# An added wait ahead of the scatters of a block loop, in a Mamba-2 and mixture-of-experts layer

## What is computed

```python
h = _layernorm(x) * (1 + cb) + sb
scores = sigmoid(h @ gate_w.T)
_, idx = top_k(scores + gate_b, 4)
w = 2.5 * scores[idx] / sum(scores[idx])
for e in range(16):
    y = y + comb[:, e] * ((silu(h @ w13[e, :128].T) * (h @ w13[e, 128:].T)) @ w2[e].T)
y = y + shared expert
x = x + gb * y
```

## Time and profile before

| | |
|---|---|
| median of 3 runs | 1903.9 us (1902.3 to 1906.38) |
| the profiled execution | 1903.56 us, its span 1901.8 us |
| PE busy | 1550.4 us, 82% of the span |
| DVE busy | 1423.9 us, 75% |
| ACT busy | 1092.2 us, 57% |
| POOL busy | 1042.6 us, 55% |
| scatters of the block loop, POOL L2270 | 272, 261.7 us busy, 962 ns each |
| POOL idle before them | 256.3 us |
| DMA engines over the span | 125 GB/s |

### The profile page before, as it was taken

The page is one execution under the profiler, slowest core; times in us unless marked ns, Lnnn a source line. Parts: engine busy times, 40 slices in busy tenths (PEclk is TensorE's granted clock), DMA queues, the critical chain, the costliest instruction groups (busy, mean ns, idle before and its releaser), DMA issues. The chain is left out here.

```text
span 1901.8 us, 35726 instructions
## 1 busy us (share of the span) xinstructions
PE 1550.4 (82%) x10562; PEld 1321.7 (69%) x10562; DVE 1423.9 (75%) x3336; ACT 1092.2 (57%) x2311; POOL 1042.6 (55%) x940
## 2 busy tenths in 40 slices
PE   6749999988888988989898894178888887875798
PEld 4337788777777777777777774067777777775565
DVE  6747899999999999999999995434444444442688
ACT  4635766767767676767676764245555545453222
POOL 2113446566666666666666666725555555554553
PEclk9879999999999999999999996589999999997899
DMA  8620011212121212122121215555555555552998
GB/s 283 211 80 32 25 49 43 79 60 79 62 80 61 80 59 72 64 71 71 61 77 62 75 56 171 187 168 157 168 155 159 154 171 149 162 152 75 373 400 322
DMA packets 149368, 238.24 MB, mean 125 GB/s; under 512 B 27792, under 2 KB 96144, under 8 KB 149008
## 3 DMA queue, kind: packets, MB, share of 16 engines
q1 hardware_dynamic: 123296, 166.20, 27.7%
q0 software_dynamic: 25344, 69.50, 9.9%
q10 hardware_dynamic: 544, 0.26, 0.0%
HBM read 128.66 MB, written 109.35 MB: 125 GB/s over the span
## 5 line engine op out<-in xcount | busy, mean ns | idle before, releaser
L2270 POOL DMA_INDIRECT ys_dram<-byo,bids x272 | 261.7, 962 | 256.3 <-DVE bids L2250 155.1
L1625 DVE SCALAR_TENSOR_TENSOR cv<-xc,convw,cv 128x256 f32<-128x256 f32 x576 | 331.0, 629 | 14.1 <-ACT xc L1476 14.1
L1105 POOL DMA_INDIRECT xs_dram<-rows,dest x256 | 264.5, 1033 | 61.5 <-issue 59.2
L2223 DVE TENSOR_TENSOR bhl<-bank,bhh 128x512 fp32r<-128x512 f32 x136 | 94.1, 692 | 195.9 <-ACT bhh L2175 185.0
L116 PE MATMUL bank<-wh,bhh 128*128 x544 | 161.0, 296 | 77.3 <-ACT bhh L2175 63.6
L2175 ACT ACTIVATE bhh<-bank 128x512 fp32r<-128x512 f32 x136 | 83.5, 614 | 185.2 <-PE bank L2108 177.3
L116 PEld LDWEIGHTS bank<-wh,bhh 128*128 128x128 f32 x544 | 103.0, 189 | 90.7 <-issue 90.7
L117 PE MATMUL bank<-wl,bhh 128*128 x544 | 154.9, 285 | 1.5 <-issue 1.5
L118 PE MATMUL bank<-wh,bhl 128*128 x544 | 154.0, 283 | 0.9 <-issue 0.9
L1945 POOL TENSOR_TENSOR state<-state,par 128x512 f32<-128x512 f32 x64 | 94.7, 1479 | 104.5 <-PE bank L1326 104.4
L116 PE MATMUL bank<-hTh,win_hi 128*128 128x256 f32 x384 | 114.5, 298 | 32.1 <-DVE xr L1745 21.4
(11 more groups left out here) (269 smaller groups left out, 5400.0 us busy)
## 6 DMA issues: line engine op xcount, KB each, us to landing
bx<-xs_dram SPq DMA_DIRECT2D x272, 129.0 KB
cy<-ys_dram SPq DMA_DIRECT2D x32, 1024.0 KB, 13.1
px<-in_x SPq DMA_DIRECT2D x16, 512.0 KB, 6.0
h_t<-phT SPq DMA_DIRECT2D x16, 512.0 KB, 3.7
hT<-h_t SPq DMA_DIRECT2D x32, 256.0 KB
xr<-in_x SPq DMA_DIRECT2D x32, 256.0 KB
x_dram<-xr SPq DMA_DIRECT2D x32, 256.0 KB
h_dram<-h SPq DMA_DIRECT2D x32, 256.0 KB
```

The costliest lines, as they stand in the source:

```text
L1105: pool.indirect_dma_start(out=xs_dram[:, :], out_offset=bass.IndirectOffsetOnAxis(ap=dest[p][:, CH * b + c, k:k + 1], axis=0), in_=rows[b] ...
L1625: dve.scalar_tensor_tensor(cv[b][:, m, :], xc[b][:, m, tap:tap + GROUP], convw[:, m, tap:tap + 1], cv[b][:, m, :], ALU.mult, ALU.add).then ...
L2223: dve.tensor_tensor(hl[u % 2][:, :, :, :].rearrange("p k n t -> p (k n t)"), XT[u % 2][:, :], hh[u % 2][:, :, :, :].rearrange("p k n t -> ...
L2270: pool.indirect_dma_start(out=ys_dram[:, :], out_offset=bass.IndirectOffsetOnAxis(ap=ids[u % XBUF][:, n:n + 1], axis=0), in_=yo[u % YBUF][ ...
```

## The change

Before the two scatters of pair `u`, GpSimd now also waits until the up product of pair u + 3 has been reported (the count on `up_ps` is then u + 4); at the end of the loop, for that of the last pair.

```diff
                 for u in range(PAIRS):
                     pool.wait_ge(yo_done, u + 1)
                     pool.wait_ge(ids_done, u + 1)
+                    pool.wait_ge(up_ps, min(u + 4, PAIRS))
                     for n in range(2):
                         pool.indirect_dma_start(
```

## The result

The changed kernel takes 1860.41 us (median of 4, 1855.22 to 1861.64) beside 1903.1 us for the kernel before (median of 4): the ratio is 0.9772, with a 95% interval from 0.9745 to 0.9799. It is 43 us faster. The prediction had said 1902.8 us, with a range down to 1884, and no change that can be told: it was wrong.

What follows compares the result with a forecast made beforehand. Bound: a POOL and ScalarE cycle in which four scatters hold TensorE's reports, 3.68 us a pair. Profiled 1903.56 - 1.8 (start) + 0.7 (end) = 1902.5, as median 1902.8 us; range 1884 to 1907.

Steps and rivals of the forecast that it cites:

- What bounds the loop: Block loop: four scatters in a row hold TensorE's reports; a cycle through POOL and ScalarE takes 3.68 us a pair, TensorE 2.79.
- The price of the condition: Before each pair's first scatter: an already met condition costs zero; upper bound 0.17 us each, up to 12 us in all.
- So in the state in which the loop runs, the added wait never holds: change 0: Pairs 33 to 125: every scatter starts at least 0.8 us behind its new condition, so these 92 pairs change by 0.
- met 0.8 us early: Pairs 33 to 125: no scatter starts less than 0.8 us behind the up product that the added wait asks for.
- second rival: Loop, after x2 loads: POOL waits for a held report, pairs run alone at 4.85 us, 1916 us in all; chance of slower 0.10.
- pair 129: End of the loop: its scatter would precede the up product it must wait for, so it comes 0.7 to 1.2 us later.
- The start of the loop: First pairs: the wait holds, scatters come 3.12 us apart for some pairs, then fours return; gain 1.8 us, carried to the end.
- even spacing: Pairs of scatters 3.12 us apart in place of fours, expected at the loop's start, ending after four pairs.
- old cycle: Loop before the change: four scatters in a row, 7.36 us from one four to the next, closing through POOL and ScalarE.
- The end of the loop: From pair 129: the scatter and the report behind it come 0.7 to 1.2 us later; the sum adds 0.7 us.
- first rival: Whole loop: pairs of scatters stay 3.12 us apart, 1828 us, or 1879 if every third runs into its predecessor; chance 0.28.
- The drift of 0.33 us per pair: Loop start: TensorE needs 2.79 us against 3.12, so up products end 0.33 us earlier each pair, ending the state after four pairs.

## Why the prediction was wrong, point by point

*What bounds the loop.* Right, as far as the runs reach. A report of TensorE that comes over 3 us late, four scatters in a row, and a cycle that closes through GpSimd and ScalarE: taking the scatters away freed 100 us, giving back one of two cost 17 and the other 86.

*The price of the condition.* Right where it is met, within what can be told: the wait for pair u + 2 has the same form and gave 1.0014, which the interval puts between 1 us less and 6 us more. Where it decides it has a price that the prediction did not see. As a wait ahead of the transfer it takes 0.77 us from release to scatter, not the 0.28 that the sum used for the start of the loop.

*"So in the state in which the loop runs, the added wait never holds: change 0."* This is the step that failed: it took the state of the kernel before for the state of the changed one. It was true of the undisturbed cycle. But "met 0.8 us early" compared each scatter with the end of the up product, and a held product is reported up to 4.7 us behind its end. At a disturbance the wait therefore holds, and from there on it holds in every cycle. The trace of before shows it at pair 13, in the scatters, the up product of pair 16, and the silu that waits for it:

```profile
1302.11 0.96 POOL L2270 DMA_INDIRECT ys_dram<-byo,bids  x1 [0.30 <-issue]
1303.37 0.96 POOL L2270 DMA_INDIRECT ys_dram<-byo,bids  x1 [0.30 <-issue]
1304.64 0.96 POOL L2270 DMA_INDIRECT ys_dram<-byo,bids  x1 [0.30 <-issue]
1309.17 0.96 POOL L2270 DMA_INDIRECT ys_dram<-byo,bids  x1 [3.57 <-DVE bids L2250]
```

```profile
1302.12 0.28 PE L118 MATMUL bank<-wh,bhl 128*128 x1
```

```profile
1307.02 0.38 ACT L2182 ACTIVATE bgs<-bank 128x256 f32<-128x256 f32 x1 [4.30 <-PE bank L118]
```

The product ended at 1302.40, so by the prediction's measure the scatter of pair 13, at 1303.37, stands 0.97 us behind its condition. The report reached ScalarE at 1307.02. There the wait would have held, and it would have cut a row of six scatters to four. The same stands at pairs 26 and 127. None of the three lies in the stretch from pair 33 to 125 on which the claim was made. The prediction applied the hold to its second rival and to pair 129, but not to its own criterion.

*The start of the loop.* Wrong in size and in what follows. The first scatters of pairs 0, 1, 3 and 5:

```profile
1261.09 0.96 POOL L2271 DMA_INDIRECT ys_dram<-byo,bids  x1 [23.88 <-PE bank L118]
...
1264.77 0.96 POOL L2271 DMA_INDIRECT ys_dram<-byo,bids  x1 [1.45 <-PE bank L118]
...
1271.73 0.96 POOL L2271 DMA_INDIRECT ys_dram<-byo,bids  x1 [2.21 <-ACT byo L2199]
...
1278.43 0.96 POOL L2271 DMA_INDIRECT ys_dram<-byo,bids  x1 [1.94 <-PE bank L118]
```

The first two stand 3.68 us apart and not 3.12; 0.49 of the 0.56 us is the 0.77 in place of the 0.28. Pairs 1 and 2 already make a four, and from pair 5 on nearly every four starts from a release. So the gain was not 1.8 us at the start, carried to the end, but 0.7 us in nearly every cycle. The end of the even spacing was taken to be the return of the old cycle. The return leads to fours, but a four that waits for a release starts the next one from that release, and not over ScalarE. The run with the wait from pair 40 on shows that the loop goes over from the old cycle too, once a row of six comes up.

*The end of the loop.* The 0.7 us that the sum adds there can't be tested. The changed kernel comes to its end in the new cycle, and its last ten scatters stand in one row, from 1697.20 on.

*The first rival.* Its direction was right and it had 0.28; the time lies between the two that it gave, 1828 and 1879. Its mechanism, even spacing, is not what the changed kernel does. It appears when the wait stands in the transfer, at 1.27 + 1.66 + 0.28 = 3.2 us, close to the 3.12 worked out. The drift of 0.33 us per pair that was to end it did not: TensorE falls in with the 3.2, its up product ending 0.9 us behind the first scatter and being held all the same, where the prediction had taken from the old cycle that everything within 1.65 us passes.

*The second rival.* It did not come: a wait that meets a held report was worth 0.7 us per cycle, where the rival had made it a cost. It had GpSimd stand and lose; but y was ready before the release (1401.11 against 1404.06), so ScalarE cost nothing on the way.

Why GpSimd's scatters in a row hold TensorE's reports, and why a hold begins at different distances from the first scatter, no run here tells.

## What to carry to other kernels

When an engine starts long after the work that it waited for had ended, compare the end of the work with the start of the waiter, and judge every condition by when it was reported, not by when it was done. In a loop with buffers, a time per turn is a cycle of waits: write it out as a sum, and ask of each change which link it replaces, and whether a single disturbance can move the loop over to the other cycle. A wait may make a kernel faster, where it starts an engine from an earlier link of the cycle, or keeps a burst of indirect transfers short; and of several waits before one transfer, the one that comes last is best written so that it stands in the transfer itself.

## What the runs showed of the hardware that was not expected

In the kernel before TensorE's reports were held for up to 4.7 us while indirect transfers from GpSimd followed each other at 1.27 us, though its work went on; with plain transfers from SyncE's queue the silu started 0.04 us behind the product, and with single scatters among them too, at a loss of 17 us in all. Held reports were let go nearly together (ScalarE ran through its next steps without standing, 1404.08 to 1404.62), 1.93 and 2.07 us behind the start of the last of four scatters, 1.7 us behind the last of two. And from a report to the scatter it took 0.77 us where the condition stood in a wait instruction ahead of the transfer, 0.28 us where it stood in the transfer.
